# Edge sort of a two-layer graph network: node blocks 17 columns apart instead of 16

## What is computed

```
edge_index = jnp.stack([src, dst])
edge_index_t = jnp.stack([src, dst], axis=1)
h = jnp.maximum(_layernorm(x, axis=-1), 0.0)
x = x + _L0_gnn_ref(h, edge_index_t, 1250, L0_gnn_W, L0_gnn_b)
h = jnp.maximum(_layernorm(x, axis=-1), 0.0)
x = x + _L1_gnn_ref(h, edge_index, edge_weight, 1250, L1_gnn_W, L1_gnn_alpha)
```

## Time and profile before

| | us |
|---|---|
| median of 3 runs | 1019.98 |
| lowest, highest | 1013.48, 1021.19 |
| profiled execution, own time | 1017.97 |
| its span | 1016.2 |
| PE busy | 972.9 (96%) |
| DVE busy | 872.2 (86%) |
| ACT busy | 775.0 (76%) |
| POOL busy | 643.0 (63%) |

### The profile page before, as it was taken

The page is one execution under the profiler, slowest core; times in us unless marked ns, Lnnn a source line. Parts: engine busy times, 40 slices in busy tenths (PEclk is TensorE's granted clock), DMA queues, the critical chain, the costliest instruction groups (busy, mean ns, idle before and its releaser), DMA issues.

```text
span 1016.2 us, 20178 instructions
## 1 busy us (share of the span) xinstructions
PE 972.9 (96%) x4719; PEld 781.0 (77%) x4720; DVE 872.2 (86%) x1747; ACT 775.0 (76%) x1650; POOL 643.0 (63%) x934
## 2 busy tenths in 40 slices
PE   5799999999799999999999999999999999999998
PEld 5477778787678887788878778878888788778776
DVE  6989988897769999999999999999999888873444
ACT  4887878778788888888888888888888776755210
POOL 2478877767477777777777777777777755530000
PEclk9689999899989999999999999999999999999999
DMA  8000000000021111111111111111111100010011
GB/s 220 4 3 4 2 4 2 4 2 3 19 62 42 44 42 41 40 42 43 41 43 42 40 40 41 43 42 41 44 41 42 31 30 30 24 42 1 21 41 40
DMA packets 35923, 35.16 MB, mean 35 GB/s; under 512 B 7778, under 2 KB 32095, under 8 KB 35876
## 3 DMA queue, kind: packets, MB, share of 16 engines
q1 hardware_dynamic: 31176, 33.95, 10.7%
q0 software_dynamic: 4416, 0.30, 1.7%
q10 hardware_dynamic: 284, 0.33, 0.1%
HBM read 30.92 MB, written 3.29 MB: 34 GB/s over the span
## 4 chain that ended last, share of the span: by engine, by line
PE 68%; DVE 2%; ACT 1%; issue 1%; POOL 0%; POOLq 0%
PE node_ps L1166 8%; PE edge_ps L1205 8%; PE edge_ps L1211 8%; PE edge_ps L1210 8%; PE edge_ps L1206 8%; PE node_ps L1167 8%; PE m_ps L1177 4%; PE psum L1309 3%; PE psum L1311 3%; PE psum L1310 3%; PE m_ps L1291 1%; PE edge_ps L1269 1%; PE edge_ps L1270 1%; PE edge_ps L1261 1%; PE edge_ps L1266 1%; PE edge_ps L1265 1%
## 5 line engine op out<-in xcount | busy, mean ns | idle before, releaser
L1398 ACT ACTIVATE msg_hi<-edge_ps 128x512 fp32r<-128x512 f32 x332 | 197.6, 595 | 60.8 <-PE edge_ps L1211 60.7
L1122 POOL TENSOR_TENSOR M<-M,pair_w 125x125 f32 x332 | 160.7, 484 | 126.9 <-DVE pair_w L1545 97.2
L1559 DVE SCALAR_TENSOR_TENSOR msg_lo<-edge_ps,msg_hi 128x512 fp32r<-128x512 f32 x332 | 223.6, 683 | 17.3 <-ACT msg_hi L1398 13.0
L417 POOL DMA_INDIRECT edge_table<-fields,row_no x136 | 170.4, 1253 | 58.2 <-issue 47.4
L844 ACT ACTIVATE lane_piece<-hot_lane,fields 125x128 fp32r<-125x128 bf16 x498 | 153.8, 392 | 12.1 <-DVE hot_lane L504 11.8
L705 PE MATMUL psum<-hot_tile,lane_piece 125*128 125x384 f32 x582 | 145.8, 373 | 9.2 <-ACT lane_piece L844 6.3
L1106 POOL TENSOR_TENSOR hot_w<-hot_d,weight_l 128x252 fp32r<-128x252 bf16 x166 | 140.0, 843 | 0.0
L1166 PE MATMUL node_ps<-msg_hi,hot_s 128*125 128x512 f32 x332 | 135.1, 407 | 0.0
L1205 PE MATMUL edge_ps<-b_hi,turned_d 125*128 x332 | 132.7, 400 | 0.7 <-ACT turned_d L1382 0.7
L1211 PE MATMUL edge_ps<-a_lo,turned_s 125*128 x332 | 131.9, 397 | 0.0
L1210 PE MATMUL edge_ps<-a_hi,turned_s 125*128 x332 | 131.4, 396 | 0.2 <-ACT turned_s L1382 0.2
(11 more groups left out here) (258 smaller groups left out, 2044.8 us busy)
## 6 DMA issues: line engine op xcount, KB each, us to landing
spread<-edge_rows SPq DMA_DIRECT2D x190, 125.0 KB
out_dram<-result SPq DMA_DIRECT2D x10, 224.0 KB
edge_table<-fields,row_no POOLq DMA_INDIRECT x136
w_in<-in_L_gnn_W_dram SPq DMA_DIRECT2D x1, 2048.0 KB, 12.7
S<-in_x_dram SPq DMA_DIRECT2D x1, 1792.0 KB
w_in<-in_L_gnn_W_dram SPq DMA_DIRECT2D x1, 1024.0 KB, 5.1
S<-in_x_dram SPq DMA_DIRECT2D x1, 448.0 KB
edge_table<-zeros SPq DMA_DIRECT2D x1, 384.0 KB, 14.9
```

The lines of the kernel that those rows point to most:

```text
L417: pool.indirect_dma_start(table_dram[:, :], bass.IndirectOffsetOnAxis(ap=row_no[:, c:c + 1], axis=0), fields[:, c, 0:TABLE_FIELDS], None). ...
L1122: pool.tensor_tensor(part, part, pair_w[h][:, j, 0, 0:BN], ALU.add).then_inc(m_added, 1)
L1398: act.activation(msg_hi[j][:], edge_ps[j][:], ACT.Relu).then_inc(hi_ready, 1)
L1559: dve.scalar_tensor_tensor(out=msg_lo[j][:], in0=edge_ps[j][:], scalar=0.0, in1=msg_hi[j][:].bitcast(F32), op0=ALU.max, op1=ALU.subtract). ...
```

## The change

Six of the stage numbers move, and the step between blocks:

```
-STEP = 16
-NORMAL_AT, TURN_AT, ROUND_AT, REST_AT, PRODUCT_AT = 2, 5, 8, 12, 13
-HI_AT, LOW_AT, LO_AT = (19, 23), (23, 26), (27, 29)
+STEP = 17
+NORMAL_AT, TURN_AT, ROUND_AT, REST_AT, PRODUCT_AT = 1, 3, 7, 11, 12
+HI_AT, LOW_AT, LO_AT = (22, 26), (24, 28), (28, 32)
```

## The result

| | before | changed |
|---|---|---|
| median, us | 1016.85 (8 runs) | 1024.76 (8 runs) |
| lowest, highest | 1013.47, 1021.53 | 1018.55, 1027.69 |
| ratio to before, 95% interval | | 1.0074 (1.0044 to 1.0103) |
| profiled execution, own time | 1017.97 | 1024.89 |
| its span | 1016.2 | 1023.2 |

The change costs 7.9 us, 0.7%. Forecast were 2.9 us less, and 1024.76 lies above the range. It is small enough to count as "within 1%", but the sign is wrong.

What follows compares the result with a forecast made beforehand. No engine was full: PE was slow in heavy columns, ACT in light ones, and PE's chain decided the sort's end. Terms summed to -2.9 us, 1017.97 to 1015.1, or 1017.0 on the median's scale; range 1009 to 1023.5.

Steps and rivals of the forecast that it cites:

- The ninth column is nearly free: Gaps between blocks' products: a ninth light column costs 0.1 to 0.25 us each, taken as 0.15, +1.4 for nine gaps.
- its sign of being wrong: Gaps without extra steps, forecast at 7.3 us: the prediction is wrong if they last over 8 us.
- Rival 4: Nothing moves: DVE bounds most gaps, a ninth column costs 0.5 to 0.6 us, eating the tail's gain; 1020 to 1021, chance 0.12.
- The tail: Behind the last product: 21 light columns instead of 29, -5.1 us, and ACT two columns further ahead, -1.3.
- Gap 3: Behind block 3's products: the counts move into those products, 10.2 us for 12.4, less 1.0 for DVE's picks; together -1.3.
- the unread part: Gap 3: ACT's 3.04 us idle before copying counts, given to "remote", end unreadable; if it stays, +0.7 instead of -1.3.
- gap 5: `slots` for chunk 3 (q = 106) moves from this gap into block 5's products: -0.8 us.
- `slots` of chunk 4 into gap 7: DVE's 3.5 us of `slots` (q = 144) falls just when the gap starts, and PE stops: +2.5 us.
- The tables into gap 8: The tables (q = 158) with ACT's 1.05 us of copies leave block 9's products for a gap where PE waits for ACT: +1.7.
- rival 3: Slower by the slots stop before block 8: PE's clock falls, +4.5 us for the clock; 1021.6 to 1023.6, chance 0.20.
- The spell that the prediction left alone: PE's lower clock in 186 to 190 us, costing about 3 us: left as it is, at nothing, -3 if it goes.
- POOL's chain: Sort's end: indirect DMAs and table read-back land by about 263 to 265, PE ends near 269; hidden unless PE gains over 7 us.

Runs made afterwards that it cites:

- later copy: ACT's copy of the counts out of PSUM placed two columns later (COPY_BACK 1 for 3); on the changed kernel 1014.78 us, ratio 1.0012.

## Why the prediction was wrong

*"The ninth column is nearly free", 0.15 each: the step that failed.* Where counts, slots and tables didn't move (0, 1, 2, 4, 6) the pieces grew by 1.9, 0.4, 1.0, 1.8 and 0.8: 1.2 us a column, 10.6 for nine in place of 1.4. The gaps themselves, from the last product to the next start, went from 7.2, 7.4, 8.5, 8.1 and 7.4 to 9.1, 8.3, 9.4, 9.5 and 8.7: all over the 8 us that the prediction had named as its sign of being wrong. I had costed a gap from ACT's lead in gap 7 alone. There I took away the hold on `a_hi` and `b_hi` and let ACT start the gap two columns ahead. But ACT was held by DVE right behind it: 14.8 us of waits for products became 11.8 more for `hot_lane`, and with the copies alone moved the time stood still (0.9996). In gap 4 of the changed kernel the prefix matmuls (L693) ride along with the placing, and there neither ACT nor the lead says how long a column takes. Columns come 0.72 us apart, and once the prefix waits for DVE, 1.0 to 1.4; the prediction's 0.53 for a light column had no prefix in it:

```profile
162.51 0.36 PE L693 MATMUL psum<-hot,before_b 128*125 128x462 bf16 x1
...
163.23 0.36 PE L693 MATMUL psum<-hot,before_b 128*125 128x462 bf16 x1
...
164.91 0.36 PE L693 MATMUL psum<-hot,before_b 128*125 128x462 bf16 x1
...
166.30 0.41 PE L693 MATMUL psum<-hot,before_b 128*125 128x462 bf16 x1 [0.51 <-DVE planes L469]
...
167.36 0.41 PE L693 MATMUL psum<-hot,before_b 128*125 128x462 bf16 x1
```

The same rows stood in the trace before (gap 4: 157.26 to 163.56, no wait of PE for ACT). A look at a second gap would have told that the formula of gap 7 does not hold there. Rival 4 named this mechanism at 0.5 to 0.6 a column; it was twice that. It is shown for gap 4, and the prefix waits for DVE in gaps 2 and 6 too (up to 0.53); in gap 0 PE waited for ACT instead (0.57 before a placing), so it isn't the price of every gap.

*The tail: right.* -7.2 for -6.4. That is 0.9 a column, but the tables left the tail too; in the profiles of steps 15 and 16, where they stay, nine columns are 6.5 us (41.7 and 35.2), 0.7 each. Either way less was saved than the nine cost between products.

*The head: -1.4, given as 0.* The first product does come a column sooner.

*Gap 3, "-1.3, or +0.7 if the unread part stays": wrong, +5.7.* The unread part was what mattered. The row with "3.04 <-remote" was the only sign, and I forecast the gap around it. ACT's wait grew to 6.93, and a second came at gap 5, forecast at -0.8, measured +4.6. Less 1.2 each for the column, the two are 7.9 us of this execution's 11.5.

*`slots` of chunk 4 into gap 7, +2.5: right in kind, too large.* The stop came, later by the drift and just as described. In the timelines of DVE, ACT and PE:

```profile
229.65 0.23 DVE L492 SCALAR_TENSOR_TENSOR row_no<-lane,tile_no 125x66 int32<-125x66 f32 x1
...
230.53 0.98 ACT L844 ACTIVATE lane_piece<-hot_lane,fields 125x128 fp32r<-125x128 bf16 x3 [1.68 <-DVE hot_lane L504]
...
231.57 0.61 PE L705 MATMUL psum<-hot_tile,lane_piece 125*128 125x384 f32 x2 [1.37 <-ACT lane_piece L844]
```

The piece grew by 2.2, of which 1.2 is the column. *The tables into gap 8, +1.7:* 1.6 less 1.2, so 0.4.

*The clock.* It fell behind gap 7 as rival 3 had it: 0.92 in 230 to 234, 0.65 in the next 4 us, behind PE's stop of 1.37. That agrees in kind with what the Trainium skill says of idle gaps ("TensorE: Matmul & The Clock Gate", "HAM oscillation"), though the waits it describes there are longer. In gap 3 it doesn't fit as well: the clock was at 0.50 in all of 138 to 142, so it had fallen by 138, and PE's stop of 2.80 began at 139.6. Before it lie only the pauses of 0.4 to 0.5 between the groups of counts. The spell behind gap 7 did not cost 4.5: all of that piece's growth is 2.2, and block 8's products began only at 236.45, when the clock was on its way up again (0.50 in 234 to 236, 0.80 in 236 to 238). Rival 3's place and fall came true, its price did not. The spell that the prediction left alone stayed, later: 0.50 in 194 to 198, over the first products of block 6 as before, with a shorter one ahead of it (0.50 in 186 to 188). In the kernel before it had fallen by 184 to 186 (0.50) though PE's records show no stop between 143 and 203.

*POOL's chain: right.* The read-back was hidden, DVE waited at the end for PE:

```profile
279.13 0.56 DVE L655 TENSOR_TENSOR raw<-raw,psum 128x384 f32<-128x384 f32 x1 [3.09 <-PE psum L705]
```

Sum in measured terms: head -1.4, nine columns +10.6, tail -7.2, late signals and their stops +7.9, `slots` and tables +1.4: +11.3 for the 11.5 of the sorts. It had to close nearly, since every term but the price of a column is read off the same two executions; in the other two executions of the changed order the late signals' term is smaller (sorts of 229.4 and 229.8 us). Against the forecast the columns are 9.2 us off, and gaps 3 and 5, at -1.3 and -0.8, are 10.0.

**What stays open.** Why PE's signals behind the counts come late in one order and not in another. It isn't density alone, it didn't move with PE's stream by 80 instructions, and three executions of the changed order (two kernels) had it in chunks 3 and 4 each time. The counts of those chunks stand there at the very end of a block's products or right behind; but single late signals also fell where they stand inside products (chunk 2, with the counts spread, at steps 15, 16 and 17, and at 16 with the stages and a later copy). That it isn't the counts' signal alone is shown for gaps 3 and 5 of the changed kernel. But PE's records end before its signals arrive and ends are modelled, so the trace can't say whether PE, its signals or the records are behind; nor does a run show whether the delay is there when nothing is recorded. Nor is it shown why the later copy helps the changed kernel (1.0012 for 1.0063 to 1.0076) and no other.

## What to carry to other kernels

Moving work past a wait gains only if the engine that waited is the one that limits: before counting the wait as a gain, ask who would hold the engine next, here DVE and the ring at once. Price a column (or any unit) in several of the places where it will stand, not in the one whose rows are easiest to read. An idle time that the trace gives to nothing you can name is a term of unknown size: when a change slides other work over it, its bounds belong in the range with their full width, and spreading or moving the work beside it is the experiment to run first; here that was worth 0.3 to 0.4% in the kernel before, more than the change could give, and nothing clear with another step.

## What was not expected of the hardware

PE's signal for 66 small matmuls (10 columns each) reached ACT 1.7 to 5.0 us after the last recorded end in the 15 of 60 cases that are late signals of over 3 us, while in 28 others it took 0.01 to 0.4 us. In gap 3 of the changed kernel PE's other signals, of products, transposes and placings, were late with it by 2.9 to 4.1 us, and one placing later by nothing. PE's records show pauses there: the last count matmuls fall into groups of 5 and 6, a group each 0.75 us, with 0.4 to 0.5 us of "issue" between. By the fit over the profiles ACT's wait costs the sort about its own length.
